# DMA transposes of the weight pieces, fp16 passes for the values-keys products, and accumulating DMAs for five tiles' y

## The reference, cut to what matters

```
xn = layernorm(x)
h  = xn @ gnn_W                      # graph convolution, then A (edge counts) times h, relu
q, k = relu(xn @ Wq + bq), relu(xn @ Wk + bk);  v = xn @ Wv + bv      # 16 heads of 64
context = q @ k^T / (l * DH);  attn = context @ v;  mix = attn @ Wo + bo
x2 = x + gnn + mix
xq = fake_quant(layernorm(x2))
h  = fake_quant(silu(xq @ wq(w_gate)^T) * (xq @ wq(w_up)^T))
out = x2 + h @ wq(w_down)^T          # wq: per-row scale, rounded to 8 bits
```

## Time and profile before

| | us |
|---|---|
| median of 3 runs (range) | 754.85 (754.16 to 755.08) |
| the profiled execution: its time | 754.69 |
| the profiled execution: span of the trace | 752.9 |
| PE busy | 718.1 (95% of the span) |
| DVE busy | 488.9 (65%) |
| ACT busy | 210.0 (28%) |
| POOL busy | 271.3 (36%) |

### The profile page before, as it was taken

One profiled execution on the slowest core, in us unless ns is written; L12 is line 12 of the kernel. 1 busy time (PEld: TensorE's weight loads), 2 busy tenths in 40 slices (PEclk: granted clock), 3 DMA queues, 4 the chain that ended last, 5 costly groups with the idle time before them and its releaser, 6 DMA issues.

```text
span 752.9 us, 12271 instructions
## 1 busy us (share of the span) xinstructions
PE 718.1 (95%) x3828; PEld 367.5 (49%) x3828; DVE 488.9 (65%) x967; ACT 210.0 (28%) x356; POOL 271.3 (36%) x403
## 2 busy tenths in 40 slices
PE   4999999999999999999999999999999999995984
PEld 2455555555555544666544444444444445443651
DVE  7878887887666655657821111657777788757667
ACT  5133234543323254455111111501101101012350
POOL 5566677897666655540100000011111111110018
PEclk9999999999999999999999999999999999997988
DMA  9653422541000000003020300321111111001506
GB/s 343 217 127 70 94 56 59 184 160 48 0 0 0 0 2 1 2 0 112 13 100 0 111 0 0 109 81 57 57 50 48 48 48 49 22 1 27 86 20 253
DMA packets 43614, 49.97 MB, mean 66 GB/s; under 512 B 27331, under 2 KB 28363, under 8 KB 43569
## 3 DMA queue, kind: packets, MB, share of 16 engines
q1 hardware_dynamic: 43568, 49.38, 21.5%
HBM read 37.96 MB, written 5.12 MB: 57 GB/s over the span
## 4 chain that ended last, share of the span: by engine, by line
PE 75%; issue 12%; DVE 5%; POOL 3%; ACT 2%; DMA 1%; DVEq 1%; POOLq 0%; SPq 0%; ACTq 0%
PE bank L511 32%; PE bank L584 14%; PE bank L715 12%; PE bank L689 10%; POOL mem L470 2%; PE bank L496 2%; PE bank L648 2%; PE bank L528 2%; DVE counts L1096 1%; ACT mem L801 1%; DMA mem<-in_L_mix_Wk 1%; DVE mem L1006 1%; DVE mem L1022 1%; DVE hot_dst L1083 0%; POOL hot_src L422 0%
## 5 line engine op out<-in xcount | busy, mean ns | idle before, releaser
L511 PE MATMUL bank<-mem 128*128 128x512 f16 x1440 | 328.6, 382 | 2.3 <-ACT mem L801 1.7
L511 PEld LDWEIGHTS bank<-mem 128*128 (+1 forms) x1440 | 138.2, 98 | 156.1 <-issue 6.0
L422 POOL TENSOR_SCALAR hot_src<-iota_p,src_col 125x128 bf16<-125x128 bf16 x252 | 174.4, 707 | 14.1 <-issue 14.1
L1096 DVE TENSOR_TENSOR counts<-bank,counts 128x120 f32 x328 | 92.4, 282 | 49.2 <-issue 8.4
L584 PE MATMUL bank<-mem 128*128 128x384 f16 (+1 forms) x576 | 107.5, 344 | 0.0
L715 PE MATMUL bank<-mem 128*128 128x512 f16 x480 | 105.4, 379 | 0.0
L689 PE MATMUL bank<-mem 128*128 128x512 f16 x400 | 88.0, 379 | 0.0
L584 PEld LDWEIGHTS bank<-mem 128*128 128x128 f16 (+1 forms) x576 | 55.3, 98 | 43.6
L715 PEld LDWEIGHTS bank<-mem 128*128 128x128 f16 x480 | 46.7, 98 | 54.3
L1217 DVE SCALAR_TENSOR_TENSOR mem<-bank,cols,mem 128x512 f32 x20 | 15.0, 751 | 81.8 <-ACT mem L881 81.8
L821 ACT ACTIVATE src_gap<-iota_p,loT 125x128 bf16<-125x128 bf16 x84 | 33.6, 400 | 115.2 <-PE bank L496 106.6
(11 more groups left out here) (153 smaller groups left out, 660.3 us busy)
## 6 DMA issues: line engine op xcount, KB each, us to landing
mem<-in_x SPq DMA_DIRECT2D x18, 512.0 KB, 3.5
out_x<-mem SPq DMA_DIRECT2D x9, 512.0 KB
mem<-in_L_mix_Wk SPq DMA_DIRECT2D x4, 1024.0 KB, 9.6
mem<-in_L_mix_Wv SPq DMA_DIRECT2D x4, 1024.0 KB, 8.3
mem<-in_L_mix_Wq SPq DMA_DIRECT2D x4, 1024.0 KB, 5.1
mem<-in_L_gnn_W SPq DMA_DIRECT2D x4, 1024.0 KB, 5.2
mem<-in_L_mix_Wo SPq DMA_DIRECT2D x2, 2048.0 KB, 7.8
mem<-in_L_ffn_w_down SPq DMA_DIRECT2D x4, 352.0 KB, 3.0
```

The source lines that it names most:

```text
L422: pool.tensor_scalar(hot_src[0:EC, i, c, :], iota_p[0:EC, :], src_col[0:EC, i, c:c + 1], None, ALU.is_equal).then_inc(S["hot_src_ready"], 1)
L511: last = pe.matmul(o[:, :], xT[:, a * K + k, bass.ds(t * P, P)], w16[i][:, k, b, :], start=(at == 0), stop=(at == len(parts) - 1))
L1096: dve.tensor_tensor(window, agg[i][:, k * WC:(k + 1) * WC], window, ALU.add).then_inc(S["adj_added"], 1)
```

## The change

Four things, each in its own place.

1. Values-keys products. `kvs` becomes two fp16 blocks (high and low), so DVE runs four more instructions, 64 partitions by 256, after the four it had. Wo is split as well: ACT writes the high part and DVE the low part of four chunks (128 by 2048), placed after units (0,4), (0,7), (1,4) and (1,6) of `g_tile` (`WO_AFTER`). A product is three fp16 matmuls in place of one fp32 one; ACT and DVE scale by 1/256 as they take it. The load of x tile 1 waits for four products more.
2. Weight pieces. The transposes on PE and the copies on ACT go. SP issues a DMA transpose for a gate or up piece and two for a down piece, when ACT's cast is done; ACT's cast of piece i waits until the transposes of piece i-2 have landed. A down piece is laid out with a pitch of 384 columns.
3. Output. For tiles 0, 2, 4, 6, 8 (`ADDED`), SP stores `x2` itself, right after the transposes of `xq`; when all five stores are done, POOL issues for each such tile an accumulating DMA that adds `y_t` to the output in memory. The others are added as before, with 256 columns on DVE and 768 on POOL (the last tile 560 and 464), and stored by SP. Each added tile has a `y_t` of its own.
4. The loops over `g_tile` units on ACT and DVE are written out.

```diff
-        kvs = part(XT + T * D, PAIRS, P)
+        kvs = part(XT + T * D, 2 * PAIRS, P, dt=F16)
+        WO_AFTER = {(0, 4): (0, 0), (0, 7): (0, 1), (1, 4): (1, 0), (1, 6): (1, 1)}
...
+            def transpose_piece(i):
+                kind, a, b = pieces[i]
+                sp.wait_ge(SF["w16_ready"], i + 1)
+                if kind == "gu":
+                    n = FR[b]
+                    sp.dma_start_transpose(wguT.rearrange("p (k m) f -> p k m f", m=2)[:, :, a, b * P:b * P + n],
+                                           raw16[i % 2][0:n, :]).then_inc(SF[f"wT_in{i % 2}"], 16)
+                else:
+                    for k in range(2):
+                        sp.dma_start_transpose(wdT[:, :, (a + k) * P:(a + k + 1) * P],
+                                               raw16[i % 2][:, k * PITCH:(k + 1) * PITCH]).then_inc(SF[f"wT_in{i % 2}"], 16)
...
+            for t in ADDED:
+                sp.dma_start(out[P * t:P * (t + 1), :], x2[:, t, :]).then_inc(SC["x2_stored"], 16)
...
+            pool.wait_ge(SC["x2_stored"], 16 * len(ADDED))
             for t in range(T):
                 s = slice(Y_DVE[t], D)
                 pool.wait_ge(SC["y_moved"], 2 * t + 2)
                 pool.wait_ge(S["consts"], 3)
-                pool.tensor_tensor(x2[:, t, s], x2[:, t, s], y_t[t % 4][:, s], ALU.add).then_inc(SC["y_ready1"], 1)
+                if t in ADDED:
+                    pool.dma_start(out[P * t:P * (t + 1), :], y_t[t], accum_op=ALU.add).then_inc(SC["y_added"], 16)
+                else:
+                    pool.tensor_tensor(x2[:, t, s], x2[:, t, s], y_t[t][:, s], ALU.add).then_inc(SC["y_ready1"], 1)
...
-                    pe.matmul(m_bank[i % 4][:, :], kvs[:, p, :], wo[n][:, p, :], start=True,
-                              stop=True).then_inc(SM["prod_full"], 1)
+                    for a, b in ((0, 0), (0, 1), (1, 0)):
+                        last = pe.matmul(m_bank[i % 4][:, :], kvs[:, a * PAIRS + p, :], wo16[n][p // 4][:, 2 * (p % 4) + b, :],
+                                         start=(a == b), stop=(a == 1))
+                    last.then_inc(SM["prod_full"], 1)
...
+            for b in range(2):
+                acc = kv_acc[b][:, :].rearrange("p (q n) -> p q n", n=P)
+                for h in range(2):
+                    r = slice(h * DH, (h + 1) * DH)
+                    dve.wait_ge(SM["kvs_hi"], 2 * b + h + 1)
+                    dve.scalar_tensor_tensor(kvs[r, PAIRS + 4 * b:PAIRS + 4 * b + 4, r], acc[r, :, r], M_UP / (N * DH),
+                                             kvs[r, 4 * b:4 * b + 4, r], ALU.mult, ALU.subtract).then_inc(SM["kvs"], 1)
```

More of the change, by code:

```diff
@@ L137, in gps_layer @@
         hq = part(H0 + FB * NP, FB, NP, dt=BF16)
-        y_t = [part(H0 + FB * NP * 3 // 2 + i * D, D) for i in range(4)]
-        assert FB * NP * 3 // 2 + 4 * D <= T * D
+        y_t = [part(XT + t // 2 * D if t in ADDED else H0 + FB * NP * 3 // 2 + t // 2 % 4 * D, D) for t in range(T)]
+        assert FB * NP * 3 // 2 + 4 * D <= T * D and len(ADDED) * D <= K * NP // 2
+        SUMMED = [t for t in range(T) if t not in ADDED]
         x_half = part(EXTRA, 4, D, dt=F16).rearrange("p (i a) d -> p i a d", a=2)
@@ L247, in gps_layer @@
         pe_slots = [(t + 1, 1) for t in range(6)] + [(6, 3), (7, 1), (8, 1), (9, 1)]
-        moves_of = [1 if kind == "gu" else 2 for kind, _, _ in pieces]
+        landed = [16 * sum(1 if kind == "gu" else 2 for kind, _, _ in pieces[i % 2:i + 1:2]) for i in range(len(pieces))]
+        PITCH = FB * P
         UNIT = [(c, b) for c in range(len(NCH)) for b in range(FB)]
@@ L872, in _, with wo_high @@
             act.activation(clip[:, 2:4], clip[:, 0:2], ACT.Exp, scale=-1.0).then_inc(SC["exp"], 1)
-            for h in range(2):
[L876 to L882, removed]
+            def wo_high(n, c):
+                act.wait_ge(SM[f"wo_in{n}"], 16)
+                act.wait_ge(SM["wo_lo"], 2 * n + c)
+                act.activation(wo16[n][c].rearrange("p (k b) n -> p k b n", b=2)[:, :, 0, :], wo[n][:, 4 * c:4 * c + 4, :], ACT.Copy,
+                               scale=W_UP).then_inc(SM["wo_hi"], 1)
+            for h in range(2):
+                for t in range(T):
+                    act.wait_ge(S["g_full"], T * h + t + 1)
+                    act.wait_ge(SM["dinv"], 3)
+                    act.activation(h16[:, t, h * HALF:(h + 1) * HALF], proj[t % 2][:, :], ACT.Copy,
+                                   scale=dinv_up[:, t:t + 1]).then_inc(S["h_hi"], 1)
+                    if (h, t) in WO_AFTER:
+                        wo_high(*WO_AFTER[h, t])
             for i in range(2 * PAIRS):
@@ L896, in piece16 @@
                 if i >= 2:
-                    act.wait_ge(SF["wT_full"], i - 1)
+                    act.wait_ge(SF[f"wT_in{i % 2}"], landed[i - 2])
+                if pieces[i][0] == "down":
+                    act.activation(raw16[i % 2][:, 0:2 * PITCH].rearrange("p (k i) -> p k i", i=PITCH)[:, :, 0:FF],
+                                   raw8[i % 2][:, 0:2 * FF].rearrange("p (k i) -> p k i", i=FF),
+                                   ACT.Copy).then_inc(SF["w16_ready"], 1)
+                    return
                 act.activation(raw16[i % 2][0:rows, 0:columns], raw8[i % 2][0:rows, 0:columns],
                                ACT.Copy).then_inc(SF["w16_ready"], 1)
[L901 to L916, removed]
+            for i in range(len(pieces)):
+                piece16(i)
             act.wait_ge(SF["drow_full"], K)
```

93 lines of the change are left out of this document (46 added, 47 removed).

## The result

The changed kernel takes 752.81 us (median of 13 runs, 751.72 to 754.03) beside 754.85 for the kernel before on the same chip (13 runs). The ratio is 0.9976, its 95% interval 0.9968 to 0.9985: faster by 2.0 us, where 6 were forecast. The time lies in the range, the direction is right, and two thirds of the gain are missing.

What follows compares the result with a forecast made beforehand. PE was taken to bound three quarters of the chain, with DVE, POOL and stores side by side at the end. 754.7 + 1.0 (start) - 2.6 (products) - 3.8 (weight pieces) - 0.6 (end) = 748.7 us; range 746.0 to 755.0.

Steps and rivals of the forecast that it cites:

- start: Start of `g_tile`: four low parts of `kvs` ahead of the first `h_lo` make PE wait once, +1.0 us.
- Wo's parts: In `g_tile`: the four chunks of Wo split by ACT and DVE fit in the units' idle time, 0.
- products: Values-keys products: three fp16 matmuls each, with DVE in a row at 0.64 us setting the pace, -2.6 us.
- weight pieces: In `tile_b`: PE is spared the pieces' transposes, -3.8 us; the DMA transposes cost 0.
- The end: Output stretch: the span ends at 752.3, set by the DMA engines, against 752.9 before, -0.6 us.
- i: At the end: POOL's time for each accumulating DMA issue, taken as 1.23 us.
- a: At the end: the DMA engines' time for each accumulation, taken as 2.2 us, the middle of 1.33 and 3.1.
- three clocks: At the end: DVE, POOL and the DMA engines, each timed separately; the later of POOL's and the engines' ends decides.
- Twice the reads: Rival at the end: reads set an accumulation's pace, a is 2.67 us, the sum 750.6; chance 0.22.
- Accumulations that choke the end: Rival at the end: read, add and write go one after another; slower by over 0.2% from a = 4.1; chance 0.12.
- lockstep: Rival at the products: PE, ACT and DVE hand over with gaps, pitch stays near 0.86 us, 751.3; chance 0.12.
- The clock: Rival near the end: the clock's fall does not come, 745.7, chance 0.06; a later rise loses up to 2 us.

Runs made afterwards that it cites:

- the part alone: The kernel before with only the output's part (five accumulating DMAs, 256 columns on DVE), with 1024 B of descriptor memory: 758.86 us, ratio 1.0066.

## Why the prediction was right and wrong

*What bounds the kernel; start, Wo's parts, products, weight pieces.* Right by mechanism and nearly by size. The stall came at the time where it was put, and once (it stands ahead of PE's third unit, which the prediction calls the second): +1.3 for +1.0, since `h_lo` began at 379.70 and not at 379.5. Wo's parts cost nothing: the second stall that they could make isn't on the timeline. The products took 11.27 us for the forecast's 12: PE sets the pace at 0.65 us (the case that I priced as "PE alone", at -3.1), since DVE needs 0.62 and not 0.64. The transposes gave 4.0 for 3.8, in each kernel that has them, and no one waited for a landing of 3.5 us.

*The step that failed is "The end", -0.6.* It reads "The later one decides", with POOL at 746.0 + 4i and the DMA engines at 743.5 + 4a. Two things were wrong with it.

First, the three clocks were taken as tied only by y and the stores. There is a fourth tie: POOL can't issue until there is room for the descriptors. With 1024 B three of these DMAs went out, and the fourth waited 4.45 us, until the third had landed (in the part alone 4.58, until 0.3 us behind the third's landing at 745.7), and everything behind it on POOL waited too: two additions and with them two plain stores. That is shown by changing the room alone: 2.2 us in the full change, 3.0 in the part alone, and the idle time gone. What isn't shown is how room is given back: the first had landed 4.3 us before the hold began, and that didn't help the fourth. The prediction named a hold among its signs of failing (POOL "held over 3.4 us for each issue"), but as a price of each issue, and the sum had no place for it. The Trainium skill (DMA: Bandwidth & Descriptors, Terms) says that GpSimd's DMAs have their descriptors written to rings in SBUF; that POOL stands still when the memory set aside for them is too small is what the runs add.

Second, a was mis-sized: 2.2 taken, 2.9 to 3.1 measured, about the upper bound. The middle of two bounds was a choice without a row; the rival that counts reads (2.67) was nearer. That a sets the end when POOL isn't held is shown by the plain stores: without the addition the same program is 5.0 us faster (3.5 by the ratios). By the formula a = 3.1 gives an end at 743.5 + 12.4 = 755.9, +3.0 against before, which is what came. The agreement is by chance, and the experiments are what show it: with the room a is 2.9, the formula gives 755.1 or +2.2, and the end is at +1.3 (27.76 against 26.47 us). So it is too dear by 0.9, and in the changed kernel the hold makes up for that. The formula had the engines in a row with nothing beside them; in the trace two queues overlap.

My i, 1.23, was a little high: 0.88 us of work, 1.10 to the start of the addition behind it. That gave back 0.5 to 1.4 us on POOL and meant nothing, because in the changed kernel and with more room the span ends 6 to 9 us behind POOL's last addition.

*The rivals.* "Twice the reads" came nearest in size: 2.1 to 2.3 times a plain store for its 2.0. That reads set the pace isn't shown. Its time, 750.6, is met by the version with enough room, 750.59, in part by luck, since a is 2.9 there and not 2.67 and the other terms moved too. For the changed kernel it is 2.2 short, by the hold. "Accumulations that choke the end" needed a of 4.1; not reached. The products did not go in lockstep. The clock between the mixing and the end shifted by little: from the mixing to the first y matmul there are 49.3 to 49.7 us in every kernel that has the products' part, and 48.9 to 49.2 in the others, a loss of 0.8 at most. In the changed kernel 0.65 of its 0.74 lie between the matmul for the largest deviation and the first transposes of `xq`, 4.00 us for 3.35: the matmul takes 0.75 for 0.46, at a granted clock of 0.50 for 1.00, and DVE then stands 0.53 us for 0.16 ahead of the first rounding. Why DVE does isn't known.

*The chances.* The case that came, faster by 0.24%, is in the 0.80, but near the edge of "same" (0.2%). It is the other parts that made it faster: the output's part is slower by itself.

## What to carry to other kernels

When work is moved from an engine into a DMA, ask what each such DMA needs besides bandwidth, and look on the issuing engine for idle time that no semaphore ends; here three went out freely, and the fourth cost a wait until the third had landed. An accumulating store is dear for the DMA engines and cheap for the compute engines: use it early in the last stretch, where the engines are idle, and stop early. Here three of ten tiles were best. Low-priority work ahead of a stage's first hand-over belongs one unit later: moving four small DVE instructions behind the second unit took 1.36 us off the stage where the clock stayed up, though the totals (1.1 and 1.3 us by the medians, 0 and 0.6 by the ratios) are too noisy to show it.

## What the runs showed of the hardware

POOL is held without any semaphore when the descriptor memory is too small: with 1024 B the fourth accumulating DMA of 128 rows x 1024 columns waited 4.45 and 4.58 us, until the third had landed, though in the changed kernel only two were in flight when the wait began; with 2048 B five went without a wait. The trace names a false releaser for it; "issue" in the chain is the sign.

An accumulating DMA of 512 KB to HBM takes 2.9 to 3.1 us of the 16 engines (3.5 in the kernel with two of them) where a plain one from the same queue takes 1.34. The median landing is 6.0 to 8.2 us where that of the plain one is 4.1.

TensorE's clock can fall to 1.2 GHz while PE is never idle: it is busy for all of 4.00 us in both windows, with one-column matmuls for 2.3 us up to 374.1. The fall came in seven of thirteen profiles and cost 1.64 us where nothing else was waiting; what decides whether it comes isn't known.
